# Function tables of ScalarE loaded by name, hidden maxima in one reduction, integers in pairs, in a one-core decoder layer

## The chip, the cores and the metric

The kernel runs on one core of one Trainium2 chip. The metric is the device time of one execution in microseconds, given as the median of three.

## What is computed

One layer over 128 sequences of 64 tokens with 128 features, in float32. It has three parts, each with a residual and a layer norm behind it. The first part is a state-space mixer: RMS norm, a projection to values, gates, keys, queries and time steps of 16 heads, a causal convolution of 4 taps, products weighted by exponentials of decay sums, and a small memory. The second is softmax attention over a context of 64 tokens with a padding mask. The third is a feed-forward part whose inputs are rounded to integers. The change concerns that part, the softmax and the decay exponentials only as far as ScalarE's function tables go.

```python
def act_quant(x):
    scale = 127.0 / clip(max(abs(x), axis=-1, keepdims=True), 1e-05)
    return clip(round(x * scale), -128, 127) / scale

h = act_quant(x) @ weight_quant(w1).T        # 128 -> 512 hidden features
h = depthwise_conv1d(h, conv_w, conv_b)      # 3 taps over the tokens
h = silu(h)
out = act_quant(h) @ weight_quant(w2).T      # 512 -> 128
```

## The kernel before

The 128 sequences are cut into 16 groups of 8 sequences, 512 tokens each. Features lie on the partitions and the 512 tokens on the free axis. The attention and the feed-forward part run late by up to three groups; the program calls their data batches. While TensorE projects group g, the attention of batch g-2 and the feed-forward part of batch g-3 are under way. The order of each engine's work is written out by hand, as calls of small functions: `fill()` for groups 0 to 3, `body(g)` for g = 4 to 11, `drain()` for groups 12 to 15 and what comes behind them. The engines wait for each other with semaphores, which the program wraps as signals (`u_ready`, `hmax_ready`, `qi_ready`, `d_mm`). Every engine works strictly in its written order, so one waiting instruction holds up all that stand behind it.

The feed-forward part of a batch d, whose 512 hidden features are four blocks of 128 (`FB`), goes like this:

- TensorE makes the up product of each block in the PSUM bank pD, ScalarE adds the bias (`ffn_bias`, L829), VectorE the taps (`ffn_taps`, L1749 and L1751, into `fa`), ScalarE applies SiLU (`ffn_silu`, L834) into `u`, a tile of 128 partitions by 4 blocks by 512 tokens.
- ScalarE takes the absolute value of each block (`hidden_abs`, L843): block 0 goes into `hm`, which is block 0 of `fa`, the others into `fa`. VectorE takes the running maximum over the blocks (`hidden_max(d, c)`, c = 1, 2, 3, L1760).
- TensorE transposes the result (`maxima_transposed`, L2484). VectorE reduces it to one maximum a token and makes the scale (`hidden_scale`, L1766 to L1769). TensorE spreads the scale over the partitions into pD (`scales_spread`, L2492).
- VectorE multiplies each block by it (L1775) and rounds to bf16 integers `qi` by adding and subtracting a large constant (L1781); both are `hidden_int(d, c)`. TensorE does the down product (`ffn_down`, L2500).

Other names that the next parts use. Of VectorE: `decayed` (L1629, a product of key-query products with the decay factors), `add_skip` (L1642), `gate_y` (L1653), `below_maximum` (L1688 and L1689, the softmax's subtraction), `softmax_sum` (L1695), `second_norm` (L1702, the attention's output and the statistics of its norm), `attention_added` (L1713, L1715). Of ScalarE: `decay_exp` (L746), `softplus_log` (L791), `attention_exp` (L879), `copy_queries` (L863, L867). TensorE's `warm()` (L2220) issues a fixed number of matmuls on constants; they stand in `fill()` and `drain()` at places where TensorE has little work.

ScalarE holds one set of function tables at a time. In the kernel before nothing in the program names a set: a load (ACT_TABLE_LOAD) is put in by the compiler where the next function is not in the set that is loaded. SiLU, the exponential and the logarithm lead to such loads.

Of the kernel before, what the change touches and what calls it, by code (L numbers as in the profile page):

```python
# [45 lines left out]
FB = FF // 128  # L46
# [79 lines left out]
def late_width(c):  # L126
    return 128 * LATE[c]
# [42 lines left out]
def build(nc, x, ctx_t, mask, norm_w, wb, wc, w_val, w_gate, w_dt, conv_w, conv_b, d_skip, a_log, dt_bias,  # L170
# [4 lines left out]
    with ctx:  # L175
# [147 lines left out]
        def sig(name, per):  # L323
            return Signal(sem(name), per)
# [52 lines left out]
        abs_ready = sig("abs_ready", FB)  # L377
        hmax_ready = sig("hmax_ready", FB - 1)
        us_ready = sig("us_ready", 1)
        qi_ready = sig("qi_ready", FB)  # L380
# [8 lines left out]
        ch_d = Chain(sem("ch_d"), 9)  # L389
# [323 lines left out]
        def _(act):  # L713
# [123 lines left out]
            def hidden_abs(d, c):  # L837

                act.wait_ge(u_ready.sem, u_ready.at(d, c + 1))
                if c == 0:  # L840
                    act.wait_ge(d_mm.sem, d_mm.at(d - 1, D_MAX))
                w = late_width(d)
                act.activation(flat(fa[:, c, 0:late_seqs(d), :]) if c else hm[:, 0:w], u[:, c, 0:w], ACT.Abs).then_inc(abs_ready.sem, 1)  # L843

# [74 lines left out]
            def fill():  # L919
# [20 lines left out]
                place_cum(0)  # L940
                memory_mask()
# [31 lines left out]
                gate_silu(1, 1)  # L973
                decay_exp(0, 5)
# [41 lines left out]
                gate_silu(2, 1)  # L1016
                decay_exp(1, 5)
# [40 lines left out]
                hidden_abs(0, 0)  # L1058
                copy_p(2, 1, 7)
                hidden_abs(0, 1)  # L1060
# [9 lines left out]
                hidden_abs(0, 2)  # L1070
# [5 lines left out]
                hidden_abs(0, 3)  # L1076
                gate_silu(3, 1)
                decay_exp(2, 5)
# [25 lines left out]
            def body(g):  # L1104
# [16 lines left out]
                hidden_abs(g - 3, 0)  # L1121
                copy_p(g - 1, 1, 7)
                hidden_abs(g - 3, 1)
# [9 lines left out]
                hidden_abs(g - 3, 2)  # L1133
# [5 lines left out]
                hidden_abs(g - 3, 3)  # L1139
                gate_silu(g, 1)  # L1140
                decay_exp(g - 1, 5)
# [26 lines left out]
            def drain():  # L1168
# [21 lines left out]
                hidden_abs(9, 0)  # L1190
# [3 lines left out]
                hidden_abs(9, 1)  # L1194
                copy_x1T(10)
                value_silu(12, 1)
                hidden_abs(9, 2)
# [5 lines left out]
                hidden_abs(9, 3)  # L1203
                gate_silu(12, 1)
                decay_exp(11, 5)
# [41 lines left out]
                hidden_abs(10, 0)  # L1247
                copy_p(12, 1, 7)
                value_silu(13, 0)
                hidden_abs(10, 1)  # L1250
# [11 lines left out]
                hidden_abs(10, 2)  # L1262
# [3 lines left out]
                hidden_abs(10, 3)  # L1266
# [43 lines left out]
                hidden_abs(11, 0)  # L1310
# [4 lines left out]
                hidden_abs(11, 1)  # L1315
# [4 lines left out]
                hidden_abs(11, 2)  # L1320
# [6 lines left out]
                hidden_abs(11, 3)  # L1327
                gate_silu(14, 1)
                decay_exp(13, 5)
# [42 lines left out]
                hidden_abs(12, 0)  # L1372
# [8 lines left out]
                hidden_abs(12, 1)  # L1381
# [4 lines left out]
                hidden_abs(12, 2)  # L1386
                copy_queries(13)
                copy_p(15, 0, 3)
                hidden_abs(12, 3)
                gate_silu(15, 1)  # L1390
                decay_exp(14, 5)
# [34 lines left out]
                hidden_abs(13, 0)  # L1426
                ffn_bias(13, 2)
                ffn_silu(13, 1)
                hidden_abs(13, 1)
# [5 lines left out]
                hidden_abs(13, 2)  # L1435
                ffn_silu(13, 3)
                copy_queries(14)
                hidden_abs(13, 3)
# [18 lines left out]
                hidden_abs(14, 0)  # L1457
                last_apply(13)
                first_apply(15)
                hidden_abs(14, 1)  # L1460
# [3 lines left out]
                hidden_abs(14, 2)  # L1464
                copy_queries(15)
                ffn_silu(14, 3)
                hidden_abs(14, 3)
# [12 lines left out]
                hidden_abs(15, 0)  # L1480
                hidden_abs(15, 1)
                hidden_abs(15, 2)
                ffn_silu(15, 3)
                hidden_abs(15, 3)
# [10 lines left out]
        def _(dve):  # L1495
# [1774 lines left out]
```

## Time and profile before

| | before |
|---|---|
| median of three executions | 873.61 us (872.51 to 873.88) |
| profiled execution, span | 869.8 us |
| TensorE busy (PE) | 830.7 us, 96% |
| ScalarE busy (ACT) | 736.7 us, 85% |
| VectorE busy (DVE) | 725.3 us, 83% |
| GpSimd busy (POOL) | 166.0 us, 19% |

The profile is one execution. Its span runs from the first instruction to the last, and the runs' times include a little outside of it; 873.61 - 869.8 = 3.8 us. Busy times are sums over an engine's instructions; matmuls overlap, so their rows add up to more than the engine's busy time. DVE is VectorE, ACT is ScalarE, PE is TensorE, and L843 is line 843 of the kernel. In a timeline a row is a run of equal instructions, with its start, its length, and in brackets how long the engine was idle before it and who ended that.

### The profile page before, as it was taken

What the parts mean: (1) busy time and instruction counts of PE and PEld (TensorE: products, weight loads), DVE (VectorE), ACT (ScalarE), POOL (GpSimd) and SP (SyncE); (2) the same over time, 40 slices, a digit from 0 to 9 for tenths busy, and PEclk for the clock granted to TensorE, in tenths of its full rate; (3) what the DMA queues carried; (4) which work ended last, traced back from release to release, by engine and by line L of the source; (5) the groups of instructions that cost most, each with busy time, mean ns of one, the idle gap of its engine ahead of it and who ended that gap; (6) DMA issues with size and microseconds to landing.
All of it is one profiled execution on the core that took longest, in us unless ns stands there. A gap on an engine that the chain in (4) does not pass through costs nothing.

```text
span 869.8 us, 21262 instructions
## 1 busy us (share of the span) xinstructions
PE 830.7 (96%) x7966; PEld 584.0 (67%) x7966; DVE 725.3 (83%) x2189; ACT 736.7 (85%) x1407; POOL 166.0 (19%) x198
## 2 busy tenths in 40 slices
PE   7899999999999999999999999999999999998874
PEld 4676767777767767777767767676767677654432
DVE  3653578989898999989898989999898988897775
ACT  3887789899898989899998989898998989784633
POOL 7101120312031131313120211312120310211110
PEclk9999999999999999999999999999999999998988
DMA  6100101010010101010100101001000000000000
GB/s 190 50 14 4 38 3 38 5 38 16 2 39 16 37 17 38 16 37 17 38 15 2 39 16 38 29 25 29 25 16 14 27 16 25 16 26 13 12 1 24
DMA packets 22403, 23.03 MB, mean 26 GB/s; under 512 B 11259, under 2 KB 13261, under 8 KB 22301
## 3 DMA queue, kind: packets, MB, share of 16 engines
q1 hardware_dynamic: 21868, 20.56, 7.8%
q8 instruction: 63, 1.03, 0.5%
q10 hardware_dynamic: 432, 1.11, 0.4%
q14 instruction: 40, 0.32, 0.1%
HBM read 16.68 MB, written 4.19 MB: 24 GB/s over the span
## 4 chain that ended last, share of the span: by engine, by line
PE 80%; ACT 7%; DVE 7%; issue 2%; DMA 1%; POOL 1%; SPq 1%; ACTq 0%; POOLq 0%; DVEq 0%
PE pM L2300 12%; PE pP L2252 8%; PE pP L2253 6%; PE pP L2254 6%; PE pDec L2287 3%; PE pY L2316 3%; PE pDec L2288 3%; PE pA L2379 3%; PE pA L2252 2%; PE pA L2351 2%; PE pC L2428 2%; PE pC L2388 2%; PE pA L2253 2%; PE pA L2254 2%; PE pD L2477 2%
## 5 line engine op out<-in xcount | busy, mean ns | idle before, releaser
L2252 PE MATMUL pP<-xn_hi,G_hi 128*128 128x256 f32 x512 | 163.0, 318 | 0.7 <-ACT P L737 0.7
L737 ACT ACTIVATE P<-pP 128x512 f32<-128x512 f32 x256 | 150.1, 599 | 7.8 <-PE pP L2254 6.6
L2253 PE MATMUL pP<-xn_lo,G_hi 128*128 128x256 f32 x512 | 143.8, 281 | 0.0
L2254 PE MATMUL pP<-xn_hi,G_lo 128*128 128x256 f32 x512 | 143.7, 281 | 0.0
L2300 PE MATMUL pM<-P,xnT 128*64 128x512 f32 x512 | 137.3, 614 | 1.9 <-DVE ML L1629 1.6
L599 POOL TENSOR_TENSOR rs_c<-ve_c,half_pow 128x4 f32<-128x4 f32 x48 | 49.1, 1023 | 405.0 <-DVE nm_c L1677 277.3
L2252 PEld LDWEIGHTS pP<-xn_hi,G_hi 128*128 128x128 f32 x512 | 96.5, 188 | 26.3 <-issue 13.9
L1629 DVE TENSOR_TENSOR ML<-pM,Lm 128x512 f32<-128x512 f32 x128 | 87.5, 684 | 22.1 <-PE pM L2300 19.2
L2253 PEld LDWEIGHTS pP<-xn_lo,G_hi 128*128 128x128 f32 x512 | 96.7, 189 | 2.9 <-issue 1.0
L2254 PEld LDWEIGHTS pP<-xn_hi,G_lo 128*128 128x128 f32 x512 | 96.5, 188 | 0.0
L746 ACT ACTIVATE Lm<-pDec 128x512 f32<-128x512 f32 x128 | 77.1, 602 | 21.3 <-PE pDec L2288 18.1
L613 POOL TENSOR_SCALAR cum<-cum,sel 48x512 bf16<-48x512 bf16 x32 | 53.2, 1671 | 182.2 <-ACT cum L820 170.9
L1587 DVE SCALAR_TENSOR_TENSOR conv<-pA,cw,conv 128x504 f32<-128x504 f32 (+2 forms) x96 | 70.2, 732 | 9.8 <-ACT conv L753 7.5
L1749 DVE SCALAR_TENSOR_TENSOR fa<-pD,fcw,fa 128x504 f32<-128x504 f32 x61 | 44.9, 736 | 13.3 <-ACT fa L829 13.2
L829 ACT ACTIVATE fa<-pD,fcb,fcw 128x512 f32<-128x512 f32 x61 | 48.1, 788 | 6.7 <-PE pD L2478 6.6
L2287 PE MATMUL pDec<-cum_diag,own_half 128*128 128x512 bf16 x128 | 49.6, 387 | 1.9 <-DMA cum_diag<-cum 1.6
L2300 PEld LDWEIGHTS pM<-P,xnT 128*64 128x64 f32 x512 | 25.6, 135 | 38.2 <-issue 22.6
L2316 PEld LDWEIGHTS pY<-ML,v_bd 128*32 128x32 f32 x2048 | 31.0, 110 | 26.6 <-issue 20.7
L2288 PE MATMUL pDec<-negR,cum 128*128 128x512 bf16 x128 | 48.5, 379 | 0.0
L1751 DVE SCALAR_TENSOR_TENSOR fa<-pD,fcw,fa 128x504 f32<-128x504 f32 x61 | 45.3, 743 | 2.2
L809 ACT ACTIVATE v_bd<-pA 64x512 f32<-64x512 f32 x64 | 37.7, 589 | 10.9 <-PE pA L2379 10.5
L2379 PEld LDWEIGHTS pA<-id_f,vT 128*64 128x64 f32 x1024 | 34.9, 138 | 16.7 <-issue 16.3
(242 smaller groups left out, 2026.1 us busy)
## 6 DMA issues: line engine op xcount, KB each, us to landing
x_in<-in_x SPq DMA_DIRECT2D x16, 256.0 KB, 3.3
cum_diag<-cum SPq DMA_DIRECT2D x256, 3.0 KB
x_res<-in_x SPq DMA_DIRECT2D x16, 256.0 KB, 2.6
ctxT<-in_ctx_t SPq DMA_DIRECT2D x16, 256.0 KB, 3.0
out_x<-r SPq DMA_DIRECT2D x16, 256.0 KB, 2.1
P<-in_wc ACTq DMA_DIRECT2D x2, 512.0 KB, 6.8
P<-in_wb SPq DMA_DIRECT2D x2, 512.0 KB, 8.6
fa<-in_w_t SPq DMA_DIRECT2D x1, 256.0 KB
```

Of the source, the lines that this page charges most:

```text
L737: act.activation(P[:, half, 2 * pair:2 * pair + 2, 0:w], pP[k % 2][:, 0:2 * w].rearrange("p (h l) -> p h l", h=2), ACT.Copy).then_inc(p_co ...
L746: act.activation(Lm[:, s % 2, :], pDec[:, :], ACT.Exp).then_inc(L_ready.sem, per_unit(g))
L1587: ins = dve.scalar_tensor_tensor(late, seqs(pA[:, 0:width(n)])[:, :, 0:L - back], cw[:, jj, K_CONV - 1 - back:K_CONV - back], late, ALU.mu ...
L1629: dve.tensor_tensor(ML[:, ml_slot(g, s), :], pM[:, :], Lm[:, s % 2, :], ALU.mult)\
L2252: pe.matmul(dst, w_hi, x_hi, start=True, stop=False)
L2253: pe.matmul(dst, w_hi, x_lo, start=False, stop=False)
L2254: return pe.matmul(dst, w_lo, x_hi, start=False, stop=True)
L2287: pe.matmul(pDec[:, :], own_half[:, :], flat(cum_diag[:, s, :, :]), start=True, stop=False)
L2288: pe.matmul(pDec[:, :], flat(cum2[g % 2][:, s, :, :]), negR[:, :], start=False, stop=True)\
L2300: last = pe.matmul(pM[64 * h2:64 * h2 + 64, :], xnT[g % 2][:, s, :], P[:, half, HH * h2:HH * h2 + HH, l0:l0 + L], start=True, stop=True)
L2316: last = pe.matmul(pY[32 * q:32 * q + 32, c0:c0 + L], v_bd[g % 2][:, s, hh, :], ML[:, ml_slot(g, s), hh * L:hh * L + L], start=True, stop= ...
L2379: last = pe.matmul(pA[64 * h2:64 * h2 + 64, 128 * k + 64 * jj:128 * k + 64 * jj + 64], vT[n % 2][:, jj, L * s:L * s + L], id_heads[:, h2], ...
```

## The change

There are three edits.

1. `exponentials()` loads the set `natural_log_exp_and_others` by its name: once at the start of ScalarE's queue, once behind `place_cum(0)`, and then once a group, ahead of the decay exponentials and the softmax's. The compiler still puts in the load for SiLU. The new order holds 38 loads where the old one has 70.
2. `hidden_abs` is gone. `hidden_max(d)` is one `tensor_reduce` of VectorE. It reads all four blocks of `u`, the blocks innermost, with absolute values, and writes `hm`. It waits for all four SiLU outputs. It stands where the last of the three maxima stood, with the exceptions that the diff shows.
3. `hidden_int(d, pair)` handles two blocks with one product and one rounding of 1024 values, the scale read twice from pD. The two pairs take the places of four single calls, in most orders the first at the place of block 0 and the second behind `attention_added`.

The orders of TensorE, SyncE and GpSimd stay as they are, except for the numbers that they wait for.

```diff
+            def exponentials():
+                act.preload_act_table_set("natural_log_exp_and_others")
+
+            exponentials()
...
-            def hidden_abs(d, c):
...
-                act.activation(flat(fa[:, c, 0:late_seqs(d), :]) if c else hm[:, 0:w], u[:, c, 0:w], ACT.Abs).then_inc(abs_ready.sem, 1)
...
-            def hidden_max(d, c):
-
-                dve.wait_ge(abs_ready.sem, abs_ready.at(d, c + 1))
-                if c >= 2:
-                    dve.wait_ge(hmax_ready.sem, hmax_ready.at(d, c - 1))
+            def hidden_max(d):
+
+                dve.wait_ge(u_ready.sem, u_ready.at(d, FB))
                 w = late_width(d)
-                dve.tensor_tensor(hm[:, 0:w], hm[:, 0:w], flat(fa[:, c, 0:late_seqs(d), :]), ALU.max).then_inc(hmax_ready.sem, 1)
+                dve.tensor_reduce(hm[:, 0:w], u[:, :, 0:w].rearrange("p c w -> p w c"), AX.X, ALU.max,
+                                  apply_absolute_value=True).then_inc(hmax_ready.sem, 1)
...
-            def hidden_int(d, c):
+            def hidden_int(d, pair):
...
-                hidden = u[:, c, 0:late_width(d)]
-                ins = dve.tensor_tensor(hidden, hidden, pD[:, 0:late_width(d)], ALU.mult)
-                if c == FB - 1:
+                w, two = late_width(d), slice(2 * pair, 2 * pair + 2)
+                hidden = u[:, two, 0:w]
+                ins = dve.tensor_tensor(hidden, hidden, pD[:, 0:w].unsqueeze(1).broadcast_to([128, 2, w]), ALU.mult)
+                if pair == FB // 2 - 1:
...
-                dve.tensor_scalar(qi[:, c, 0:late_width(d)], hidden, MAGIC, MAGIC, ALU.add, ALU.subtract)\
+                dve.tensor_scalar(qi[:, two, 0:w], hidden, MAGIC, MAGIC, ALU.add, ALU.subtract)\
...
-                hidden_max(g - 3, 1)
-                hidden_max(g - 3, 2)
                 decayed(g - 1, 4)
-                hidden_max(g - 3, 3)
+                hidden_max(g - 3)
                 below_maximum(g - 2)
                 add_skip(g - 1, 0)
                 decayed(g - 1, 5)
...
                 decayed(g - 1, 6)
                 hidden_int(g - 3, 0)
+                decayed(g - 1, 7)
+                attention_added(g - 2)
                 hidden_int(g - 3, 1)
-                decayed(g - 1, 7)
-                hidden_int(g - 3, 2)
-                attention_added(g - 2)
-                hidden_int(g - 3, 3)
                 third_norm(g - 2)
...
-                hidden_max(10, 2)
                 below_maximum(11)
-                hidden_max(10, 3)
+                hidden_max(10)
                 add_skip(12, 0)
...
-                hidden_max(12, 1)
-                hidden_max(12, 2)
                 add_skip(14, 0)
-                hidden_max(12, 3)
+                hidden_max(12)
                 below_maximum(13)
...
                 hidden_int(13, 0)
-                hidden_int(13, 1)
-                hidden_int(13, 2)
                 attention_added(14)
                 decayed(15, 7)
-                hidden_int(13, 3)
+                hidden_int(13, 1)
                 third_norm(14)
```

In the closing part the orders show how the pieces stand. The first place is VectorE's queue around the last maxima of batch 13. Before, as the program is issued:

```order
L1760 TENSOR_TENSOR fa<-fa 128x512
L1629 TENSOR_TENSOR ML<-pM,Lm 128x512
L1642 SCALAR_TENSOR_TENSOR yd<-vT,dsk,pY 128x256 x2
L1760 TENSOR_TENSOR fa<-fa 128x512
L1688 TENSOR_REDUCE mx<-pC 128x4
L1689 TENSOR_TENSOR vv<-pC,mx 128x4x64
L1629 TENSOR_TENSOR ML<-pM,Lm 128x512
L1653 TENSOR_TENSOR Yg<-yd,gT 128x2x256
```

and in the changed kernel:

```order
L1600 TENSOR_TENSOR ML<-pM,Lm 128x512
L1613 SCALAR_TENSOR_TENSOR yd<-vT,dsk,pY 128x256 x2
L1729 TENSOR_REDUCE fa<-u 128x512
L1659 TENSOR_REDUCE mx<-pC 128x4
L1660 TENSOR_TENSOR vv<-pC,mx 128x4x64
L1600 TENSOR_TENSOR ML<-pM,Lm 128x512
L1624 TENSOR_TENSOR Yg<-yd,gT 128x2x256
```

The two short maxima (L1760) have become one reduction (L1729) behind the two instructions of `add_skip` (L1642, now L1613) and still ahead of `below_maximum(14)`, whose reduction of scores (L1688, now L1659) is the softmax's first step.

The second place is VectorE's queue from the softmax's sum of batch 15 on, with the integers of batch 14. Before:

```order
L1695 TENSOR_REDUCE sw<-ew 128x4
L1696 RECIPROCAL sw<-sw 128x4
L1775 TENSOR_TENSOR u<-u,pD 128x512
L1781 TENSOR_SCALAR qi<-u 128x512
L1702 SCALAR_TENSOR_TENSOR o<-pC,sw,bo_b 128x128 x4
L1501 BN_STATS st_c<-o 128x6 x4
L1503 MEMSET pad 128x1
L1505 BN_AGGR mv_c<-st_c 128x2 x4
L1707 TENSOR_SCALAR ve_c<-mv_c 128x4
L1708 TENSOR_SCALAR nm_c<-mv_c 128x4
L1775 TENSOR_TENSOR u<-u,pD 128x512
L1781 TENSOR_SCALAR qi<-u 128x512
```

and in the changed kernel:

```order
L1666 TENSOR_REDUCE sw<-ew 128x4
L1667 RECIPROCAL sw<-sw 128x4
L1673 SCALAR_TENSOR_TENSOR o<-pC,sw,bo_b 128x128 x4
L1472 BN_STATS st_c<-o 128x6 x4
L1474 MEMSET pad 128x1
L1476 BN_AGGR mv_c<-st_c 128x2 x4
L1678 TENSOR_SCALAR ve_c<-mv_c 128x4
L1679 TENSOR_SCALAR nm_c<-mv_c 128x4
L1746 TENSOR_TENSOR u<-u,pD 128x1024
L1752 TENSOR_SCALAR qi<-u 128x1024
```

One block's product and rounding (L1775, L1781) stood ahead of the attention's output (L1702) and three behind its statistics; now nothing of the integers stands ahead of it (L1673), and both pairs (L1746, L1752) stand behind.

The third place is ScalarE's queue in the closing part, between the SiLU outputs of batch 14 and the exponentials of the softmax of batch 15. Before:

```order
L829 ACTIVATE fa<-pD,fcb,fcw 128x512
L863 ACTIVATE vv<-pC 128x512
L834 ACTIVATE u<-fa 128x512
L843 ACTIVATE fa<-u 128x512
L867 ACTIVATE qT<-pC,bq_s 128x512
L834 ACTIVATE u<-fa 128x512
L843 ACTIVATE fa<-u 128x512
L879 ACT_TABLE_LOAD
L879 ACTIVATE ew<-vv 64x4x64 x2
```

and in the changed kernel:

```order
L833 ACTIVATE fa<-pD,fcb,fcw 128x512
L859 ACTIVATE vv<-pC 128x512
L838 ACTIVATE u<-fa 128x512
L863 ACTIVATE qT<-pC,bq_s 128x512
L838 ACTIVATE u<-fa 128x512
L719 ACT_TABLE_LOAD
L875 ACTIVATE ew<-vv 64x4x64 x2
```

The absolute values (L843) are gone, and the table load carries the line of `exponentials()` (L719) and stands at the same place, behind the last SiLU.

## Rows read from the trace of the kernel before

**Rows 1.** Windows, three stretches: PE, PEld, DVE, ACT, POOL busy; clock, DMA, GB/s

```profile
45.00:750.00 705.00, 702.73 (x7109) 504.41 (x7108) 611.64 (x1837) 644.85 (x1238) 131.78 (x150) 1.00 0.08 23
750.00:800.00 50.00, 44.20 (x363) 27.15 (x362) 44.27 (x143) 31.64 (x60) 6.29 (x10) 0.93 0.06 17
800.00:870.00 70.00, 47.24 (x247) 26.64 (x245) 47.14 (x146) 32.99 (x60) 7.23 (x12) 0.86 0.03 12
```

**Rows 2.** Waits of TensorE, 740 to 870 us: total, times, longest

```profile
PE pC L2325 <- ACT x L884: 0.9, 1, 0.9
PE pC L2446 <- ACT qT L867: 0.8, 1, 0.8
```

**Rows 3.** ScalarE's groups by line and shape: busy, mean ns, idle before

```profile
L843 ACT ACTIVATE fa<-u 128x512 f32<-128x512 f32 x64 | 40.7, 639 | 0.1
...
L746 ACT ACT_TABLE_LOAD x30 | 38.5, 1283 | 0.5
...
L791 ACT ACT_TABLE_LOAD x16 | 20.5, 1283 | 0.3
L834 ACT ACT_TABLE_LOAD x16 | 20.5, 1283 | 0.3
```

**Rows 4.** VectorE's groups by line and shape, the same columns

```profile
L1775 DVE TENSOR_TENSOR u<-u,pD 128x512 f32<-128x512 f32 x64 | 43.3, 677 | 1.7 <-PE pD L2492 1.7
L1760 DVE TENSOR_TENSOR fa<-fa 128x512 f32<-128x512 f32 x48 | 32.9, 686 | 2.4 <-ACT fa L843 1.1
...
L1781 DVE TENSOR_SCALAR qi<-u 128x512 bf16<-128x512 f32 x64 | 27.6, 430 | 2.2
...
L1695 DVE TENSOR_REDUCE sw<-ew 128x4 f32<-128x512 f32 x16 | 10.9, 681 | 0.9 <-ACT ew L879 0.9
...
L1688 DVE TENSOR_REDUCE mx<-pC 128x4 f32<-128x256 f32 x16 | 6.8, 422 | 2.7 <-PE pC L2449 1.8
```

**Rows 5.** Timeline of VectorE in a loop group: start, busy time

```profile
296.55 1.48 DVE L1760 TENSOR_TENSOR fa<-fa 128x512 f32<-128x512 f32 x2
...
298.55 0.68 DVE L1760 TENSOR_TENSOR fa<-fa 128x512 f32<-128x512 f32 x1
```

**Rows 6.** Timeline of TensorE in the same group

```profile
300.28 0.66 PE L2484 MATMUL pD<-id_f,fa 128*128 128x128 f32 x4
```

**Rows 7.** Timeline of VectorE, last maxima of batches 10 and 12

```profile
637.18 0.68 DVE L1760 TENSOR_TENSOR fa<-fa 128x512 f32<-128x512 f32 x1
...
734.52 0.69 DVE L1760 TENSOR_TENSOR fa<-fa 128x512 f32<-128x512 f32 x1
```

**Rows 8.** Timeline of TensorE, the transpositions of these two

```profile
638.74 0.60 PE L2484 MATMUL pD<-id_f,fa 128*128 128x128 f32 x4
...
735.44 0.66 PE L2484 MATMUL pD<-id_f,fa 128*128 128x128 f32 x4
```

**Rows 9.** Timeline of VectorE, 775 to 781 us

```profile
775.75 0.86 DVE L1642 SCALAR_TENSOR_TENSOR yd<-vT,dsk,pY 128x256 f32<-128x256 f32 x2
...
777.58 0.42 DVE L1689 TENSOR_TENSOR vv<-pC,mx 128x256 f32<-128x256 f32 x1
```

**Rows 10.** Timeline of TensorE, two places between 775 and 795 us

```profile
779.10 0.66 PE L2325 MATMUL pC<-id_f,ew 128*128 128x128 f32 x4
...
791.27 1.89 PE L2500 MATMUL pD<-w,qi 128*128 128x128 bf16 x16 [0.40 <-DVE qi L1781]
```

**Rows 11.** Timeline of VectorE, 817 to 832 us

```profile
818.99 0.68 DVE L1760 TENSOR_TENSOR fa<-fa 128x512 f32<-128x512 f32 x1
...
824.15 1.12 DVE L1702 SCALAR_TENSOR_TENSOR o<-pC,sw,bo_b 128x128 f32<-128x128 f32 x4 [0.18 <-PE pC L2461]
```

**Rows 12.** Timeline of TensorE, 817 to 833 us

```profile
819.73 0.67 PE L2484 MATMUL pD<-id_f,fa 128*128 128x128 f32 x4 [1.66 <-DVE fa L1760]
```

**Rows 13.** Timeline of VectorE, 850 to 861 us

```profile
852.26 0.69 DVE L1760 TENSOR_TENSOR fa<-fa 128x512 f32<-128x512 f32 x1 [0.21 <-ACT fa L843]
```

**Rows 14.** Timeline of TensorE, 849 to 861 us

```profile
855.78 4.65 PE L2220 MATMUL pM<-warm_src 128*128 128x512 bf16 x16
```

More of the change, by code:

```diff
@@ L376, in build @@
         u_ready = sig("u_ready", FB)
-        abs_ready = sig("abs_ready", FB)
-        hmax_ready = sig("hmax_ready", FB - 1)
+        hmax_ready = sig("hmax_ready", 1)
         us_ready = sig("us_ready", 1)
-        qi_ready = sig("qi_ready", FB)
+        qi_ready = sig("qi_ready", FB // 2)
         ve3_ready = sig("ve3_ready", 1)
@@ L388, in build @@
         ch_c = Chain(sem("ch_c"), 13)
-        ch_d = Chain(sem("ch_d"), 9)
+        ch_d = Chain(sem("ch_d"), 7)
         ch_l = Chain(sem("ch_l"), 2)
@@ L940, in fill @@
                 place_cum(0)
+                exponentials()
                 memory_mask()
@@ L973, in fill @@
                 gate_silu(1, 1)
+                exponentials()
                 decay_exp(0, 5)
@@ L1016, in fill @@
                 gate_silu(2, 1)
+                exponentials()
                 decay_exp(1, 5)
@@ L1075, in fill @@
                 copy_p(3, 0, 3)
-                hidden_abs(0, 3)
                 gate_silu(3, 1)
+                exponentials()
                 decay_exp(2, 5)
@@ L1138, in body @@
                 copy_p(g, 0, 3)
-                hidden_abs(g - 3, 3)
                 gate_silu(g, 1)
+                exponentials()
                 decay_exp(g - 1, 5)
@@ L1202, in drain @@
                 copy_p(12, 0, 3)
-                hidden_abs(9, 3)
                 gate_silu(12, 1)
+                exponentials()
                 decay_exp(11, 5)
@@ L1265, in drain @@
                 copy_p(13, 0, 3)
-                hidden_abs(10, 3)
+                exponentials()
                 decay_exp(12, 5)
@@ L1326, in drain @@
                 copy_p(14, 0, 3)
-                hidden_abs(11, 3)
                 gate_silu(14, 1)
+                exponentials()
                 decay_exp(13, 5)
@@ L1385, in drain @@
                 ffn_silu(12, 3)
-                hidden_abs(12, 2)
                 copy_queries(13)
                 copy_p(15, 0, 3)
-                hidden_abs(12, 3)
                 gate_silu(15, 1)
+                exponentials()
                 decay_exp(14, 5)
@@ L1434, in drain @@
                 copy_x1T(14)
-                hidden_abs(13, 2)
                 ffn_silu(13, 3)
                 copy_queries(14)
-                hidden_abs(13, 3)
+                exponentials()
                 decay_exp(15, 5)
@@ L1463, in drain @@
                 ffn_silu(14, 2)
-                hidden_abs(14, 2)
                 copy_queries(15)
                 ffn_silu(14, 3)
-                hidden_abs(14, 3)
+                exponentials()
                 attention_exp(15)
@@ L1896, in fill @@
                 hidden_int(0, 0)
+                decayed(2, 7)
+                attention_added(1)
                 hidden_int(0, 1)
-                decayed(2, 7)
-                hidden_int(0, 2)
-                attention_added(1)
-                hidden_int(0, 3)
                 third_norm(1)
@@ L2032, in drain @@
                 hidden_int(10, 0)
+                decayed(12, 7)
+                attention_added(11)
                 hidden_int(10, 1)
-                decayed(12, 7)
-                hidden_int(10, 2)
-                attention_added(11)
-                hidden_int(10, 3)
                 third_norm(11)
@@ L2066, in drain @@
                 cum_low(14)
-                hidden_max(11, 3)
+                hidden_max(11)
                 below_maximum(12)
@@ L2119, in drain @@
                 hidden_int(12, 0)
+                decayed(14, 7)
                 hidden_int(12, 1)
-                decayed(14, 7)
-                hidden_int(12, 2)
-                hidden_int(12, 3)
                 attention_added(13)
@@ L2495, in ffn_down @@
             def ffn_down(d):
[L2496 removed]
+                pe.wait_ge(qi_ready.sem, qi_ready.at(d, FB // 2))
                 d_turn(d, D_Y)
```

69 lines of the change are left out of this document (9 added, 60 removed).

## Prediction

> **What bounds the kernel now.** I read the table of stretches first. From 45 to 750 us TensorE is busy 702.73 of 705 us at full clock, while ScalarE has 644.85 and VectorE 611.64 [rows 1]. So 15 of the 16 groups run at TensorE's pace, and work taken from another engine is worth at most the 2.3 us that TensorE stands idle there, unless it makes TensorE wait where it does not wait now. After 750 it is different: TensorE is idle for 5.8 us up to 800 and for 22.8 us behind that. The next question is who ends these waits. The chain of waits and the list of waits name VectorE for most of it, ScalarE only for pieces under 1 us such as 0.9 and 0.8 us [rows 2]. So the change must be priced as latency: how much earlier or later VectorE and ScalarE release TensorE at the places where it stands close behind them.
>
> **What the change takes away, in busy time.** ScalarE: 64 absolute values of 639 ns, 40.7 us, and 32 of 70 table loads of 1.283 us (70 are the 30, 16 and 16 of the rows and 8 single ones; the new order holds 38), 41.1 us [rows 3]. VectorE: 48 maxima of 686 ns (32.9 us), 64 products of 677 and 64 roundings of 430 (70.9 us) [rows 4].
>
> The Trainium skill (ScalarE: Activation LUTs, What ACT_TABLE_LOAD costs) gives 2.66 us for every switch of the set, 1.28 us of load and 1.38 us of drain, so 85 us instead of 41 us would be saved. The trace has only the load itself, 1.283 us, and the next activation starts right behind it, so the row decides; nothing below hangs on this.
>
> **What it adds.** One reduction reads 2048 values a partition, the four blocks of one token side by side, and writes 512. The trace has reductions of 512 values at 681 ns and of 256 at 422 ns, thus 1.01 ns a value and 163 ns fixed; 2048 values give 163 + 2071 = 2.24 us [rows 4]. That every value lies 2 KB from the one before it no row shows. From below: the fastest access here is the rounding, (430 - 163)/512 = 0.52 ns a value, which gives 1.2 us. From above: if such reads go at half the rate of the reductions' rows, 163 + 4142 = 4.3 us; the factor two is within what two forms of access of this engine already differ by. I take 2.24 us, because the reductions' rows are the same operation and their price does not depend on how many values go into one result. A pair of products (1024 values) comes to 163 + 2 x (677 - 163) = 1.19 us and its rounding to 163 + 2 x 267 = 0.70 us, so two pairs take 3.8 us and the four singles took 4.4 us. VectorE in sum: 33 + 71 off, 16 x 2.24 + 16 x 3.78 on, 8 us less. Its throughput hardly changes; what changes is that the maxima no longer hide behind the SiLU outputs that come one by one. Three short operations, two of them done while the last block is still on its way, become one long one that starts only when all four blocks are there.
>
> **The loop (groups 4 to 11, and batch 0).** The two early maxima and the last one start at 296.55 and 298.55 [rows 5]. With the two gone, the decay product between them is done at 297.2 and the reduction runs from there to 299.4, 0.2 us later than now. TensorE comes to the transposition of the maxima at 300.28 [rows 6], so 0.8 us of cover are left (1.0 now). All of it holds as long as the reduction stays under 3.0 us. Behind it the integers in pairs win back 0.6 us before the product that needs them. ScalarE, freed of 5 us a group, only waits more. **Term: 0.**
>
> **Batches 9 to 12.** The order in the closing part is written out, and there VectorE reaches the reduction without having won anything from the removed early maxima, since it waits for a product of TensorE just ahead of it. Batch 10: the last maximum starts at 637.18, behind `below_maximum`; the reduction ends at 639.45, and TensorE is there at 638.74 [rows 7, 8]: 0.75 us of wait. Batch 12: `add_skip` needs TensorE's product, now and then, and can move up only by the 0.9 us to the end of that product; the reduction runs from about 733.5 to 735.8 against 735.44: 0.4 us [rows 7, 8]. Batches 9 and 11, the same way, 0.1 and 0.4 us. **Term: +1.7 us**, and about 0.5 us off because ScalarE is earlier at a few of TensorE's short waits.
>
> **Batch 13.** The order puts the reduction ahead of `below_maximum(14)`, behind `add_skip(15, 0)`, which ends at 776.6 because TensorE's product does [rows 9]. It ends at 778.8 where the maximum ended at 777.2, and everything behind is later by 1.5 us: the softmax's subtraction ends at 779.5 instead of 778.0, the exponentials (two of 0.41 us) at 780.4, and TensorE, which starts to transpose them at 779.10 now [rows 9, 10], does it at 780.4. ScalarE's earlier table load does not help, since the subtraction is now the later of the two. From there TensorE and VectorE follow each other without cover: the product, the norm, `decayed(15, 7)`, the integers. The pairs don't give it back: the new order puts two blocks' products, 1.9 us, behind the attention sum where one block's 1.1 us stood. TensorE's `ffn_down(13)`, which waits 0.40 us for the integers now and starts at 791.27 [rows 10], starts at 792.7. **Term: +1.4 us.** Behind it come 12 warming matmuls in fixed number, so it is not absorbed.
>
> **Batch 14.** TensorE has the transposition of the maxima ahead of the softmax's, and waits 1.66 us for it already [rows 12]. The maximum starts at 818.99 [rows 11]; the reduction instead ends at 820.95 rather than 819.68, +1.3 us. The product of the attention and the norm at 824.15 [rows 11] shift by the same. Of the integers one block was done before this norm, in an idle gap; now both pairs stand behind it, 3.8 us where 3.25 us stood ahead of the attention sum. **Term: +1.7 us**, which runs through the third norm, the quantisation and the up products of batch 15.
>
> **Batch 15.** ScalarE's three absolute values between the third and fourth SiLU go away, so the last SiLU ends at 850.9 (when the taps are done), not 851.6. The reduction then runs to 853.2; the last maximum runs from 852.26 to 852.95 [rows 13]. The integers then win 0.6 us, but 16 warming matmuls stand ahead of the last down product, from 855.78 to 860.43 [rows 14], and cover exactly that. **Term: +0.2 us.**
>
> Start: the loads at the head of ScalarE's queue and in the mask of the memory lie beside weight transfers and the moves of the decay sums, for which TensorE waits until 41 us: 0.
>
> Sum: 0 + 1.7 - 0.5 + 1.4 + 1.7 + 0.2 = +4.5 us on a span of 869.8 us, so 874.3. The runs' median, 873.61, lies 3.8 us above the span (what is outside of it doesn't change): 878.1 us, slower by 0.5%. About 0.2% (1.7 us) is what a measurement of this kernel can tell from no change.
>
> **Rivals.**
> *Reads with a gap cost double (slower, much more).* The reduction takes 4.3 us. In the loop it ends at 301.5 and TensorE waits 1.2 us in each of batches 0 to 8, 11 us; batches 9 to 12 add 2.1 us each to their 1.7, batches 13 to 15 2.1 us each to their 3.3: 30 us, 904 us. It decides from 3.0 us on. Against it: nothing in the rows; for it: nothing either, so it keeps a fifth. The Trainium skill (Advanced Engine Details and Errata, SBUF Cachelines) speaks for it: it asks for two hits on a 16-byte line for full performance, and here successive values lie in different lines; it gives no figure, and no row here shows such a read. Chance 0.18, part of it with a milder penalty, between 883 and 893.
>
> *The tail hides it (no change).* TensorE's clock is not full behind 800 us, mean 0.86 [rows 1], so a part of it runs at 1.2 instead of 2.4 GHz. If the moved waits put a slow piece into a wait, 3 us are given back and the result is 874 to 875 us. Chance 0.16.
>
> *Relief wins (faster).* The reduction costs near its lower bound, 1.2 us. Then batch 13 is about level, batch 14 gains the integers' part or nothing, batches 9 to 12 lose nothing, the last reduction ends 0.8 us sooner, and ScalarE's lead ends the small waits of [rows 2]: 2 to 3 us less, 871 us. It decides below 1.5 us. The same sign comes if the ScalarE waits are worth more than I think, since ScalarE gives up 11% of its work. Chance 0.20.
>
> *The forecast*: 0.46, with its own range of 875.5 to 882.
>
> The set loaded by name could in principle lack a function and be loaded again by the compiler; the order shows 38 loads and no second one beside a named one, so I give that none.
>
> **How the numbers follow.** Slower by over 0.2%: forecast and doubled reads, 0.46 + 0.18 = 0.64. Within 0.2%: 0.16. Faster: 0.20. The range 871 to 893 leaves out the full doubling (0.12) and the fastest part of the relief (0.07).
>
> **What would show it.** The reduction's row: 2.2 us if I am right, 4.3 for the doubled reads, 1.2 for relief. Table loads 38 of 1.28 us, ScalarE near 655 us busy, VectorE near 717. TensorE's busy share from 45 to 570 us unchanged; its wait at the transposition of the maxima new in batches 10 and 12, the attention's transposition of batch 14 later by 2.7 us (1.4 + 1.3), `ffn_down(14)` by 3.1 (1.4 + 1.7). The prediction is wrong if the tail behind 775 us comes out no longer than now, or if TensorE gets idle in the loop.

## The result and the profile after

The changed kernel takes 898.34 us (median of 4, 897.79 to 900.13) where the kernel before takes 873.06 us (median of 4, 871.81 to 873.88): a ratio of 1.030, 95% interval 1.0287 to 1.0313. It is 3% slower. Forecast were 878.1 us and at most 893. The profiled execution has a span of 896.0 us, 26.2 more than before.

The groups of VectorE of the kernel after, by line and shape (busy us, mean ns of one, idle time before):

```profile
L1729 DVE TENSOR_REDUCE fa<-u 128x512 f32<-128x2048 f32 x16 | 59.6, 3726 | 0.7 <-ACT u L838 0.7
...
L1746 DVE TENSOR_TENSOR u<-u,pD 128x1024 f32<-128x1024 f32 x32 | 38.8, 1212 | 1.2 <-PE pD L2427 1.2
...
L1752 DVE TENSOR_SCALAR qi<-u 128x1024 bf16<-128x1024 f32 x32 | 22.2, 694 | 1.1
```

The reduction takes 3726 ns, not 2.24 us. The pairs are as forecast: 1212 and 694 ns against 1.19 and 0.70 us worked out from [rows 4]. Of ScalarE's 38 table loads these two groups hold 35, the same view:

```profile
L719 ACT ACT_TABLE_LOAD x19 | 24.4, 1283 | 2.5 <-issue 2.1
L838 ACT ACT_TABLE_LOAD x16 | 20.5, 1283 | 0.3
```

The windows by stretch, as [rows 1] has them for before, with one more stretch behind (the changed kernel's span is longer):

```profile
45.00:750.00 705.00, 686.78 (x6842) 496.60 (x6901) 614.13 (x1726) 576.33 (x1132) 121.90 (x146) 1.00 0.07 22
750.00:800.00 50.00, 43.45 (x466) 29.45 (x467) 44.89 (x113) 36.19 (x67) 7.92 (x10) 0.99 0.06 18
800.00:870.00 70.00, 51.27 (x301) 31.09 (x305) 51.18 (x163) 28.76 (x55) 9.00 (x14) 0.86 0.02 8
870.00:896.00 26.00, 12.19 (x58) 6.12 (x56) 15.26 (x30) 7.21 (x14) 1.21 (x2) 0.78 0.05 20
```

TensorE is busy 686.78 us of the 705 where it was 702.73. VectorE's busy time there has hardly moved (614.13 against 611.64), although 2% fewer groups pass in the stretch, and ScalarE has given up 68.5 us. Who ends TensorE's waits is in the list of waits (total us, times, longest):

```profile
PE pD L2419 <- DVE fa L1729: 23.5, 15, 5.3
...
PE pC L2260 <- ACT ew L875: 3.2, 1, 3.2
PE pD L2435 <- DVE qi L1752: 2.8, 2, 1.4
```

15 of the 16 transpositions of the maxima (L2419, before L2484) wait, 23.5 us together; before only those of batches 14 and 15 did, 5.0 us together. Batch 13's does not wait because TensorE has stood 3.2 us for the softmax's weights (ScalarE's `ew`) just ahead of it. In the timeline of TensorE, a group of the loop ([rows 6] shows the one of before) and batch 12 ([rows 8]), 14 ([rows 12]) and 15:

```profile
305.26 0.66 PE L2419 MATMUL pD<-id_f,fa 128*128 128x128 f32 x4 [0.73 <-DVE fa L1729]
...
753.16 0.66 PE L2419 MATMUL pD<-id_f,fa 128*128 128x128 f32 x4 [1.81 <-DVE fa L1729]
...
842.77 1.12 PE L2419 MATMUL pD<-id_f,fa 128*128 128x128 f32 x4 [4.52 <-DVE fa L1729]
...
878.58 1.11 PE L2419 MATMUL pD<-id_f,fa 128*128 128x128 f32 x4 [5.25 <-DVE fa L1729]
```

How far the changed kernel has fallen behind at the start of the same transposition, from the two timelines: 2.2 us at batch 0 (156.1 and 158.3 us), 9.5 at batch 8 (540.6, 550.2), 17.7 at batch 12, 20.3 at 13, 23.0 at 14, 25.6 at 15, and 26.2 at the end. So a group of the loop takes 48.98 us in place of 48.07, batches 9 to 12 lose 2.0 each, the three behind them 2.6 each, and 0.6 come at the very end.

### The profile page after: what moved, and what is told of

Its sections match the earlier page's. It is cut to its first block, busy times and chain, and to the rows that moved or that the text cites. A ratio compares the mean times of both kernels' runs of the same rounds, so it can differ in the third digit from the quotient of the medians.

```text
span 896.0 us, 20949 instructions
## 1 busy us (share of the span) xinstructions
PE 829.1 (93%) x7894; PEld 588.5 (66%) x7966; DVE 746.5 (83%) x2093; ACT 671.2 (75%) x1311; POOL 160.8 (18%) x198
## 3 DMA queue, kind: packets, MB, share of 16 engines
q8 instruction: 63, 1.03, 0.5%
## 4 chain that ended last, share of the span: by engine, by line
PE 73%; DVE 17%; ACT 4%; issue 3%; DMA 1%; SPq 1%; POOL 1%; ACTq 0%; POOLq 0%; DVEq 0%
PE pM L2235 12%; PE pP L2187 7%; DVE fa L1729 7%; PE pP L2188 5%; PE pP L2189 5%; PE pDec L2223 4%; PE pA L2314 3%; PE pY L2251 3%; PE pC L2363 2%; PE pA L2286 2%; PE pC L2323 2%; PE pC L2396 2%; PE pDec L2222 2%; PE pC L2334 2%; PE pC L2324 2%
## 5 line engine op out<-in xcount | busy, mean ns | idle before, releaser
L612 POOL TENSOR_SCALAR cum<-cum,sel 48x512 bf16<-48x512 bf16 x32 | 50.1, 1574 | 199.1 <-ACT cum L824 187.7
L1729 DVE TENSOR_REDUCE fa<-u 128x512 f32<-128x2048 f32 x16 | 59.6, 3726 | 0.7 <-ACT u L838 0.7
```

What stands on the lines that cost most here:

```text
L1729: dve.tensor_reduce(hm[:, 0:w], u[:, :, 0:w].rearrange("p c w -> p w c"), AX.X, ALU.max, apply_absolute_value=True).then_inc(hmax_ready.se ...
```

## Experiments

Each kernel was measured beside the kernel before on the same chip; ratios are to that. Its medians in these measurements were 872.4 to 873.5 us. Short edits are shown as diffs against the kernel that each starts from.

### One part at a time

Three kernels put one part each into the kernel before. The first has only `exponentials()` and its calls:

```diff
+                exponentials()
                 decay_exp(g - 1, 5)
```

> The kernel before with the named tables alone (38 loads; absolute values, short maxima and single integers stay). My theory from the traces: the loop and the closing part gain nothing, since TensorE does not wait for ScalarE there, and the start loses about 1.4 us: the memory mask is ready earlier, TensorE has done its matmuls by 38.2 us and then stands until the moved decay sums land at 41 us, 2.7 instead of 1.6 us, and goes on at 1.2 GHz for a while. So 874 to 875 us, first transposition of the maxima at 157.5 instead of 156.1. Rival: the slow piece at the start is chance, no difference, 873 +- 0.5. Rival: relief of ScalarE wins, under 872.

Measured: 871.93 us, ratio 0.9984 (0.9975 to 0.9993). It is faster, by 1.1 us, where a loss was expected. Of the expected slower start a part is there. TensorE waits 2.5 us for the moved decay sums (the DMA `cum_diag<-cum`) where it waited 1.6 before; the twelve profiles with named tables have 2.3 to 2.8 us there, the three without 1.6 to 1.9. It is not all of the start: the first transposition of the maxima is late in this profile (158.7 us), but also, by less, in that of the pairs alone (157.3), which has all the old loads, and the wait for an input transfer near 10 us (`P<-in_wb`) lies between 2.8 and 5.5 us in the profiles with named tables and between 3.1 and 4.3 in the three without. The stretch up to 45 us, of the tables alone, then of the pairs alone:

```profile
0.00:45.00 45.00, 35.26 (x238) 25.49 (x243) 20.98 (x64) 21.84 (x44) 20.83 (x26) 0.90 0.41 116
```

```profile
0.00:45.00 45.00, 37.29 (x241) 25.76 (x245) 21.28 (x64) 26.34 (x49) 20.71 (x26) 0.92 0.41 116
```

The granted clock (third figure from the end, 0.90 and 0.92) is below the 0.96 of the kernel before in both, so the lower clock comes without the tables too. The medians say that the tables give more than the start costs. Between the profiles of before and after the start makes 1.5 of the 26.2 us (2.2 us at the first transposition, less its own new wait of 0.7). What the tables give comes in the loop: a group takes 47.98 us instead of 48.07, although no row shows TensorE waiting for ScalarE there.

The second has only `hidden_int` in pairs, in the changed kernel's order:

```diff
                 hidden_int(g - 3, 0)
-                hidden_int(g - 3, 1)
                 decayed(g - 1, 7)
-                hidden_int(g - 3, 2)
                 attention_added(g - 2)
-                hidden_int(g - 3, 3)
+                hidden_int(g - 3, 1)
```

> The kernel before with the integers in pairs alone, in the changed kernel's order. Theory: loop unchanged (0), a loss of 0 to 1.5 us in batches 13 and 14, where a block's integers stood in an idle gap ahead of the norm: 873 to 874.5. Rival: VectorE's saved 0.5 us a batch counts, 872 or less.

Measured: 872.87 us, ratio 1.000 (0.9991 to 1.0008). As the theory had it: `ffn_down(13)` starts 0.8 us later than the work around it and 1.0 us is given back at the next stage; `ffn_down(14)` starts 1.3 us later (831.39 against 830.10 us), and 1.1 us of it are back at the warming matmuls behind the up products of batch 15 (845.28 against 845.12).

The third has only the reduction, with `hidden_abs` gone:

```diff
-                hidden_max(g - 3, 1)
-                hidden_max(g - 3, 2)
                 decayed(g - 1, 4)
-                hidden_max(g - 3, 3)
+                hidden_max(g - 3)
```

> The kernel before with the one reduction alone (no absolute values on ScalarE; table loads and single integers as before). Theory: it carries nearly all of the loss: the reduction takes 3.73 us, TensorE waits 0.7 to 0.8 us at the transposition of the maxima in each of batches 0 to 8, 1.5 to 2 in 9 to 12, 3 and more behind; 895 to 898. Rival: most comes only with the tables or the pairs (VectorE's and ScalarE's orders out of step): under 885.

Measured: 897.76 us, ratio 1.0285 (1.0272 to 1.0299). The reduction alone makes 24.8 of the 25.3 us that the whole change costs. A group of the loop takes 49.15 us, 1.08 more than before; the other two parts give 0.17 of it back in the changed kernel.

### Why the reduction is slow

Three kernels change only what the reduction reads: 2048 values and 512 results each time, the same waits and the same order, but over other values, so that they no longer compute the reference's function. In the first, four neighbouring values are reduced:

```diff
-                dve.tensor_reduce(hm[:, 0:w], u[:, :, 0:w].rearrange("p c w -> p w c"), AX.X, ALU.max,
+                dve.tensor_reduce(hm[:, 0:w], u[:, :, :].rearrange("p c w -> p (c w)").rearrange("p (w c) -> p w c", c=FB), AX.X, ALU.max,
```

> The changed kernel with the reduction over four neighbouring values in place of the four blocks' values of one token: the same 2048 values read, 512 written, the same waits, but other maxima. If the 2 KB step between reads makes the reduction slow: 2.24 us as predicted for it, TensorE without waits in the loop, 878 to 881. If the price lies in the 512 short groups of four (or in the absolute value): 3.7 us and 898 as now.

In the other two the four values lie 16 and 8 bytes apart (k = 4 and k = 2):

```diff
+                dve.tensor_reduce(hm[:, 0:w].rearrange("p (a k) -> p a k", k=4), u[:, :, :].rearrange("p c w -> p (c w)").rearrange("p (a c k) -> p a k c", c=FB, k=4), AX.X, ALU.max,
```

> The changed kernel with the reduction over values that lie 16 bytes apart in place of 2 KB (other maxima; the same 2048 reads, 512 results, waits). If any step to another 16-byte line costs (as the Trainium skill, Advanced Engine Details and Errata, SBUF Cachelines, has it): about 3.7 us for one, as with 2 KB, and 898 us. If only far steps cost: 2.28 us as with neighbours, and 874 to 875.

> The same with values 8 bytes apart, so that two reads in a row fall into one piece of 16 bytes. If two reads in one line are enough: 2.28 us and 874 to 875. If every step that is not to the neighbour costs: 3.7 us and 898.

| step between reads | one reduction | kernel | ratio |
|---|---|---|---|
| 4 bytes | 2277 ns | 874.67 us | 1.0025 (1.0015 to 1.0035) |
| 8 bytes | 2277 ns | 876.8 us | 1.0052 (1.0035 to 1.0069) |
| 16 bytes | 3794 ns | 902.48 us | 1.0348 (1.0328 to 1.0369) |
| 2 KB (the change) | 3726 ns | 898.34 us | 1.030 (1.0287 to 1.0313) |

The rows of VectorE's groups, for 4 bytes and then for 16:

```profile
L1729 DVE TENSOR_REDUCE fa<-u 128x512 f32<-128x2048 f32 x16 | 36.4, 2277 | 0.7 <-ACT u L838 0.7
```

```profile
L1729 DVE TENSOR_REDUCE fa<-u 128x512 f32<-128x2048 f32 x16 | 60.7, 3794 | 0.7 <-ACT u L838 0.7
```

With 163 ns fixed, a value costs 1.03 ns at 4 and 8 bytes, and 1.74 to 1.77 ns at 16 bytes and 2 KB. The absolute value and the short groups of four are the same in all of them and cost next to nothing: 2277 ns are 40 more than [rows 4] gave. If two reads within one line are enough, these steps leave only lines of 16 bytes: with lines of 8 bytes the step of 8 would have been slow, with lines of 32 the step of 16 fast.

This is what the Trainium skill (Advanced Engine Details and Errata, SBUF Cachelines) states: lines of 16 bytes, full speed from two hits on a line on. It gives no figure; here the price of a line for every value is a factor of 1.7.

The kernels' times follow in the main, 875 and 877 us against 898 and 902. Within each pair they differ by more than the reduction does. Between 4 and 8 bytes (2.1 us) the profiles have the difference ahead of the first transposition (156.2 and 159.0 us), where nothing was changed. Of the 4.1 us between 2 KB and 16 bytes, 68 ns a reduction explain 1.1; the profiles have 1.7 ahead of the first transposition, and why the closing part differs too stays open.

### Where VectorE's longer reduction becomes 0.9 us a group

The changed kernel with TensorE's transposition of the maxima one step later in the loop:

```diff
-                maxima_transposed(g - 3)
                 head_pair(g, 0, 5)
+                maxima_transposed(g - 3)
```

> The changed kernel, and in the loop (batches 1 to 8) TensorE transposes the maxima behind the next pair of projections in place of ahead of it, which gives the reduction some 0.7 us more of cover. If the loss in the loop is a late release at this one place: the wait of 0.73 us goes away there, 8 x 0.8 = 6 us back, 892. If it is VectorE's sum of work, or the wait turns up at the next place: 897 to 898.

Measured: 897.34 us, ratio 1.0292 (1.0272 to 1.0312). The wait moved. So both places of TensorE were given more cover:

```diff
-                maxima_transposed(g - 3)
                 head_pair(g, 0, 5)
                 decay(g - 1, 6)
-                weights_transposed(g - 2)
+                maxima_transposed(g - 3)
                 head_pair(g, 0, 6)
+                weights_transposed(g - 2)
                 decay(g - 1, 7)
-                attend(g - 2)
                 scales_spread(g - 3)
+                attend(g - 2)
```

> The changed kernel with cover at both places in the loop (batches 1 to 8): TensorE transposes the maxima and, one step further on, the softmax's weights later, and spreads the scales ahead of the attention product. When only the first was moved, the same 0.73 us turned up at the second. If the loop's loss is lateness at these two places: 6 us back, 892, and TensorE's busy time from 205 to 550 us full. If VectorE's work in sum or a third place limits: 897 as with the first alone.

Measured: 902.36 us, ratio 1.035 (1.0331 to 1.0369), slower than the changed kernel itself. VectorE now waits in addition for the attention product, which stands behind the scales in TensorE's order (7.1 us in 7 waits between 200 and 560 us), and a group takes 49.6 us. Next, the reduction was let start earlier:

```diff
-                rms_stats(g + 1)
                 cum_low(g)
                 decayed(g - 1, 4)
                 hidden_max(g - 3)
                 below_maximum(g - 2)
+                rms_stats(g + 1)
```

> The changed kernel, and in the loop (batches 1 to 8) the statistics of the next group's RMS norm, 1.6 us of VectorE, stand behind the softmax's subtraction in place of ahead of the reduction, which can then start when the last SiLU is done, 1.35 us earlier. It takes nothing off VectorE's sum and gives no cover on TensorE's side. If the loop's loss is the late start of this one chain (reduction, subtraction): it ends 303.85 where TensorE is there at 304.5, no wait at the transposition of the maxima and none at the softmax's weights, 8 x 0.9 = 7 us back, 891. If VectorE's sum of work limits: 898.

Measured: 898.95 us, ratio 1.0308 (1.0283 to 1.0333). And last, `rms_stats(g + 1)` behind `second_norm(g - 2)`:

> As the kernel before this one, but the statistics of the next group's RMS norm (1.6 us) stand behind the attention's norm, so outside the stretch from the last taps to the scale, in which VectorE runs without idle time and which ends in three things that TensorE waits for (maxima, softmax's weights, scale). If the loop's loss is the length of this stretch: all three waits go, 8 x 0.9 = 7 us back against the changed kernel, 891 to 892. If VectorE's sum of work over the whole group limits, a wait turns up behind it (integers, norms) and it stays at 897 to 899.

Measured: 894.33 us, ratio 1.0281 (1.021 to 1.0352). The interval holds the 1.030 of the changed kernel, but only because one of the four executions took 905.5 us, at a granted clock of 0.925; the other three took 893.4 to 894.6, below all four of the changed kernel (897.8 to 900.1). So this order probably gives back some 4 us, where the expectation's two cases were 7 and none. In the profile 1.8 us of it lie in the loop (from the first to the ninth transposition 390.05 us instead of 391.85, 0.2 a group), and 1.35 ahead of it, where nothing was changed. TensorE's waits between 200 and 560 us (total, times, longest), of the changed kernel, then of these four in the order told:

```profile
PE pD L2419 <- DVE fa L1729: 5.9, 8, 0.7
```

```profile
PE pC L2260 <- ACT ew L875: 4.6, 8, 0.6
```

```profile
PE pP L2187 <- ACT P L741: 10.1, 8, 1.3
```

```profile
PE pD L2427 <- DVE us L1739: 8.5, 8, 1.1
```

```profile
PE pM L2235 <- DVE ML L1600: 7.1, 8, 0.9
```

Each time eight waits, one a group, and each time at another place: the maxima, the softmax's weights, ScalarE's copies (in ScalarE's order they stand behind the softmax's exponentials, which wait for VectorE's subtraction), the scale, the next decay product. VectorE's own waits in the same loop show why, of the changed kernel and then of the one before (200 to 550 us):

```profile
DVE xq_lo L1714 <- ACT xq_hi L829: 8.7, 7, 1.3
DVE fa L1720 <- ACT fa L833: 3.5, 7, 0.5
```

```profile
DVE xq_lo L1743 <- ACT xq_hi L825: 8.1, 7, 1.2
DVE fa L1749 <- ACT fa L829: 4.2, 7, 0.6
DVE o L1702 <- PE pC L2461: 3.0, 8, 0.4
```

In the timeline of VectorE these two are all that a group of after has:

```profile
284.81 0.74 DVE L1720 SCALAR_TENSOR_TENSOR fa<-pD,fcw,fa 128x504 f32<-128x504 f32 x1 [0.49 <-ACT fa L833]
...
330.85 0.69 DVE L1714 TENSOR_TENSOR xq_lo<-pD,xq_hi 128x512 fp32r<-128x512 f32 x1 [1.26 <-ACT xq_hi L829]
```

From the taps (284.81 us) to 1.26 us ahead of `xq_low` (330.85) VectorE waits for nobody: 45 us in a row out of 49. Before, it waited once more in between, 0.4 us a group for the attention product (L1702), and the maxima were done 1.05 us before TensorE came ([rows 5, 6]). The reduction has used up both, and what is left over appears wherever TensorE next needs VectorE. The sums agree: a group less VectorE's waits is 45.9 us before (48.07 less 2.1) and 47.2 after (48.98 less 1.7). So VectorE has 1.3 us more to do in a group, 0.4 of it come out of its waits, and 0.9 lengthen the group. Moving work within the 45 us moves TensorE's wait; the best of the four orders took 0.2 of the 0.9 us off, the others nothing.

### The forecast's price, made real

To have a kernel that computes the reference with reads of 8 bytes, two blocks' SiLU outputs were laid side by side value by value:

```diff
+        def two_blocks(pair):
+            return u[:, 2 * pair:2 * pair + 2, :].rearrange("p c w -> p (c w)").rearrange("p (w b) -> p w b", b=2)
...
-                act.activation(u[:, c, 0:late_width(d)], flat(fa[:, c, 0:late_seqs(d), :]), ACT.Silu)\
+                act.activation(two_blocks(c // 2)[:, 0:late_width(d), c % 2], flat(fa[:, c, 0:late_seqs(d), :]), ACT.Silu)\
...
-                dve.tensor_reduce(hm[:, 0:w], u[:, :, 0:w].rearrange("p c w -> p w c"), AX.X, ALU.max,
+                tokens = u[:, :, :].rearrange("p c w -> p (c w)").rearrange("p (a w b) -> p w a b", a=2, b=2)
+                dve.tensor_reduce(hm[:, 0:w], tokens[:, 0:w, :, :], AX.XY, ALU.max,
```

> The changed kernel with two blocks' SiLU outputs laid side by side, value by value (ScalarE writes every other value, 8 bytes apart; the reduction reads two neighbours, then two more 4 KB on; the product runs straight through; the rounding reads 8 bytes apart). By what 8 bytes apart cost: reduction 2.28 us, SiLU, product and rounding as now (0.63, 1.21, 0.70 us), 875 to 877. Rival: ScalarE or the rounding pays for the 8 bytes (each 0.3 us or more longer), 877 to 885. Rival: the jump of 4 KB costs even with two reads on each side, 3 us and 885 or more.

Measured: 875.8 us, ratio 1.0041 (1.0028 to 1.0054), and 23 us less than the change. The groups of its VectorE and ScalarE:

```profile
L841 ACT ACTIVATE u<-fa 128x512 f32<-128x512 f32 x64 | 42.7, 672 | 1.7 <-DVE fa L1725 1.3
...
L1733 DVE TENSOR_REDUCE fa<-u 128x512 f32<-128x2048 f32 x16 | 36.4, 2277 | 0.7 <-ACT u L841 0.7
```

The reduction is down to 2277 ns, though after two neighbours comes a jump of 4 KB. ScalarE's write of every other value takes 672 ns; the same SiLU into neighbouring places takes 627 in the changed kernel:

```profile
L838 ACT ACTIVATE u<-fa 128x512 f32<-128x512 f32 x64 | 39.9, 627 | 1.9 <-DVE fa L1722 1.7
```

Product and rounding are unchanged (1210 and 695 ns).

The same with two orders of the closing part turned:

```diff
                 add_skip(15, 0)
-                hidden_max(13)
                 below_maximum(14)
+                hidden_max(13)
...
                 hidden_max(14)
-                hidden_scale(14)
                 softmax_sum(15)
+                hidden_scale(14)
...
-                maxima_transposed(14)
                 weights_transposed(15)
+                maxima_transposed(14)
```

> The interleaved layout, and in the closing part two orders turned: batch 13's reduction behind the softmax's subtraction of batch 14, and for batch 14 the softmax's weights transposed and summed ahead of the maxima. If the closing part's loss comes from the reduction standing ahead of the softmax there: 2.5 to 3 us less than the interleaved kernel, 872 to 874. If the chain of the integers is the later one anyway: no gain, within 1 us of it.

Measured: 875.98 us, ratio 1.0042 (1.0029 to 1.0054): no gain. The softmax's transposition of batch 14 comes 1.3 us earlier than in the interleaved kernel (779.08 against 780.35), but TensorE's waits for the scale (L2431 <- L1743) have grown from 0.9 to 2.6 us; the chain of the maxima was about as late as the softmax.

### Without the reduction

The kernel before with the named tables and the pairs, absolute values and short maxima kept:

> The kernel before with the named tables and the pairs, and the absolute values and the three short maxima as before. The tables alone gave 1.1 us, the pairs alone nothing: 872 us if they add up; 870 or less if ScalarE's and VectorE's relief help each other; 873 or more if the pairs spoil what the tables give.

Measured: 871.33 us, ratio 0.9992 (0.998 to 1.0003). The two add up to no more than the tables alone. Of all kernels run, the tables alone are the only ones faster beyond their interval.

## Why the prediction was wrong

**The step that failed** is the price of the reduction: "I take 2.24 us, because the reductions' rows are the same operation and their price does not depend on how many values go into one result". The reason is right and was beside the point; what decides is the step between reads, and it measured 3.73 us. The bounds, 1.2 and 4.3 us, held it. The choice between them did not: the reductions' rows all read values side by side, so the nearest row was no evidence on this, and the one source that spoke of it, the Trainium skill (Advanced Engine Details and Errata, SBUF Cachelines), spoke for the dear end. "Reads with a gap cost double" got 0.18, and the range stopped at 893.

**The mechanism of that rival was right.** It said that the loop holds up to 3.0 us and that TensorE waits for what is above. At 3.73 us that makes 0.73 us a group, and the timeline has 0.73; TensorE idle in the loop was also the prediction's own sign of being wrong. Worked through with 3.73 us its sum is 9 x 0.73, plus 1.7 + 4 x 1.5 for batches 9 to 12, plus 3.3 + 3 x 1.5 for 13 to 15, less 0.5, 21.6 us or 895.2 us, already above the 893 that the range allowed for a milder penalty. Measured are 26.2 us between the spans. Of the rest about 1.5 us are the start, which the prediction put at 0 (TensorE's wait for the decay sums alone went from 1.6 to 2.7 us), 1.5 us the loop's 0.92 a group in place of 0.73, and 1.7 us lie in the closing part.

**The terms at the forecast's own price** can be read from the kernel with neighbouring reads, 2277 ns. Its TensorE at the transpositions of batches 10, 12 and 14, at the softmax's weights of batch 14 and at `ffn_down(13)`:

```profile
637.48 0.66 PE L2419 MATMUL pD<-id_f,fa 128*128 128x128 f32 x4 [0.60 <-DVE fa L1729]
...
734.85 0.66 PE L2419 MATMUL pD<-id_f,fa 128*128 128x128 f32 x4 [0.39 <-DVE fa L1729]
...
779.30 0.66 PE L2260 MATMUL pC<-id_f,ew 128*128 128x128 f32 x4 [1.73 <-ACT ew L875]
...
791.58 1.89 PE L2435 MATMUL pD<-w,qi 128*128 128x128 bf16 x16 [1.43 <-DVE qi L1752]
...
821.53 1.11 PE L2419 MATMUL pD<-id_f,fa 128*128 128x128 f32 x4 [3.18 <-DVE fa L1729]
```

- Loop: no wait, as forecast. But the term is not 0: a group takes 47.88 us, 0.19 less than before, 1.5 us over the eight, and the tables alone give 0.09 a group of it. "At most the 2.3 us that TensorE stands idle there" looked in the wrong place: before, TensorE is shown busy for all of 200 to 550 us, and these groups got shorter all the same. Laid over the group of before that starts at 300.28 us, this kernel wins 0.09 us at the first up product (330.21, whose `xq_hi` ScalarE writes) and 0.12 at a projection into pP (345.55, which ScalarE's copies have to empty first); the profile names a wait at neither.
- Batches 10 and 12: 0.60 and 0.39 us of wait, forecast 0.75 and 0.4. Batches 9 to 12 together lose 0.8 us, forecast 1.2 (1.7 less 0.5).
- Batch 13: the softmax's weights 1.6 us later against the stage ahead, forecast 1.4.
- Batch 14: 1.5 us at the maxima (from 1.66 to 3.18), forecast 1.3, and 1.35 more until `ffn_down(14)` (830.10 and 833.25 us), 2.9 in all against 1.7. Of this 0.9 comes back at the up products of batch 15, which take longer before (from 842.15 to 845.12) than here (845.16 to 847.20).
- Batch 15: 0.6 us at the maxima, of which 0.2 is given back at the last down product, forecast 0.2 in all.
- Sum: the span is 872.2 us, 2.4 more than before, forecast 4.5; medians 1.7 us apart. So even at its own price of the reduction the forecast was 2 to 3 us too high, above all by the loop.

**The other rivals.** "Relief wins": ScalarE's relief is worth 1.1 us (tables), the reduction's lower bound was never near. "The tail hides it": a part comes back, 1.0 us of batch 13 and 1.1 of batch 14 with the pairs alone; in the changed kernel far from all.

**Pairs and table loads** cost what was worked out: 1212 and 694 ns, and 38 loads of 1283 ns. ScalarE's busy time came to 671.2 us all the same, not near 655. With the reduction alone it fell from 736.7 to 711.2, by 25.5 us for the absolute values and not by the 40.7 of their row: in ScalarE's timeline an activation begins about 0.1 us before the one ahead has ended ([rows 3] counts both in full), so taking one out frees less than its row says. No term of the sum hung on this.

## What to carry to other kernels

Before a reduction is fed through a rearranged view, look at the distance between the values that it reads one behind the other: at 8 bytes in float32 it ran at the price of neighbouring values, at 16 bytes and at 2 KB at 1.7 times that. Where the trace has no row of that access, price the change at both ends and ask what each would do; here an arrangement with two neighbours a line kept the price and cost ScalarE 45 ns a write. An engine that waits for nobody over most of a loop's round is a bound too, whatever its busy share: count the slack where others meet it, and expect that work moved inside that stretch mostly moves the wait (here at best 0.2 of 0.9 us a group came off).

## What was not expected of the hardware

- 2048 values reduced into 512 took 2277 ns at steps of 4 and 8 bytes, 3794 at 16 bytes, 3726 at 2 KB; a jump of 4 KB after every second value cost nothing.
- ScalarE wrote 512 float32 values 8 bytes apart in 672 ns, side by side in 627.
- Up to 45 us the granted clock was 0.96 in two profiles and 0.90 to 0.92 in the others, and the first transposition of the maxima came between 156.1 and 160.0 us.
- With TensorE shown busy throughout, a group of the loop could still get 0.2 us shorter when ScalarE had less to do, at two places where TensorE takes over from ScalarE and the profile shows no wait.
- ScalarE's activations overlap by about 0.1 us, so 64 of 639 ns each took 25.5 us of its busy time, not 40.7.
